# A gated state-space and expert layer on one core: adapter products on 128 rows, with mixed adapter values in unused rows of the down input

## What is computed

```
def _fused_linear(x, W, qa, qb, scale, w):
    out = x @ W.T
    a = jnp.einsum('th,krh->tkr', x, qa)
    b = jnp.einsum('tkr,khr->tkh', a, qb)
    mix = jnp.einsum('tkh,tk->th', b, w)
    return out + scale[None, :] * mix

def expert(muW, gW, gqa, gqb, gs, uW, uqa, uqb, us, dW, dqa, dqb, ds, w):
    xe = x + w @ muW.T
    gate = jax.nn.silu(_fused_linear(xe, gW, gqa, gqb, gs, w))
    up = _fused_linear(xe, uW, uqa, uqb, us, w)
    return _fused_linear(gate * up, dW, dqa, dqb, ds, w)
```

## Time and profile before

| | us |
|---|---|
| median of three runs | 1694.26 |
| lowest and highest run | 1688.27, 1695.64 |
| span of the profiled execution | 1685.8 |
| PE busy in it | 1568.4 |
| DVE busy | 1155.5 |
| POOL busy | 737.8 |
| ACT busy | 617.2 |

### The profile page before, as it was taken

How to read it: one execution, slowest core, us unless ns; L and a number is a source line. 1 busy time by engine, 2 the same in 40 slices (tenths; PEclk the granted TensorE clock), 3 DMA queues, 4 the chain that set the end, 5 groups by cost and what they waited for, 6 DMA issues and landing times.

```text
span 1685.8 us, 19547 instructions
## 1 busy us (share of the span) xinstructions
PE 1568.4 (93%) x6856; PEld 1155.1 (69%) x6856; DVE 1155.5 (69%) x1634; ACT 617.2 (37%) x971; POOL 737.8 (44%) x537
## 2 busy tenths in 40 slices
PE   3787799798888999999999999999999999999999
PEld 2343377566666677777777777777777777777776
DVE  5798964788999867487888755778888553333333
ACT  5545443444454434443343244333433321111111
POOL 4488510489898801077777301376786000000000
PEclk8799999899999999999999999999999999999999
DMA  7688627688787664765667445587665456566552
GB/s 251 215 285 315 254 80 253 201 290 297 270 289 286 253 255 172 248 228 205 232 238 258 152 161 196 202 275 257 238 208 180 175 200 210 184 222 222 195 181 85
DMA packets 111473, 375.87 MB, mean 223 GB/s; under 512 B 20176, under 2 KB 45776, under 8 KB 94864
## 3 DMA queue, kind: packets, MB, share of 16 engines
q1 hardware_dynamic: 101904, 340.81, 57.8%
q10 hardware_dynamic: 9472, 33.82, 5.8%
HBM read 304.33 MB, written 70.25 MB: 222 GB/s over the span
## 4 chain that ended last, share of the span: by engine, by line
PE 63%; DVE 18%; issue 5%; ACT 5%; POOL 4%; DMA 3%; SPq 0%; ACTq 0%; DVEq 0%; POOLq 0%
PE b_g L735 14%; PE b_u L735 14%; PE b_u L826 7%; DVE ring L1493 4%; PE b_g L826 3%; PE b_q L781 3%; PE b_q L826 3%; PE b_g L799 2%; DVE ring L1499 2%; PE b_g L766 2%; DVE tt L1467 2%; POOL ring L1392 2%; PE b_g L759 1%; POOL yx L1401 1%; DVE z L1467 1%
## 5 line engine op out<-in xcount | busy, mean ns | idle before, releaser
L1392 POOL TENSOR_TENSOR ring<-du,rep 128x512 f32<-128x512 f32 x256 | 344.5, 1349 | 151.4 <-DVE du L1571 91.9
L735 PE MATMUL b_g<-xnb,gm 128*128 128x512 f32 (+1 forms) x1440 | 356.2, 396 | 0.9 <-DVE xnb L1470 0.9
L735 PE MATMUL b_u<-xnb,gm 128*128 128x512 f32 (+1 forms) x1440 | 349.1, 391 | 0.0
L1493 DVE TENSOR_TENSOR_SCAN ring<-b_a,ring 128x512 f32<-128x512 f32 x256 | 310.8, 1214 | 15.7 <-ACT b_a L964 8.4
L1401 POOL TENSOR_TENSOR yx<-yx,ring 128x512 f32<-128x512 f32 x192 | 261.8, 1364 | 130.4 <-DVE ring L1499 129.9
L735 PEld LDWEIGHTS b_g<-xnb,gm 128*128 128x128 f32 (+1 forms) x1440 | 252.1, 179 | 89.1 <-issue 24.6
L735 PEld LDWEIGHTS b_u<-xnb,gm 128*128 128x128 f32 (+1 forms) x1440 | 257.1, 179 | 71.1
L1467 DVE SCALAR_TENSOR_TENSOR tt<-tt,b_g 128x512 f32<-128x512 f32 (+1 forms) x120 | 82.1, 684 | 222.7 <-ACT tt L964 222.5
L964 ACT ACTIVATE b_a<-delta,a_neg 128x512 f32<-128x512 f32 x256 | 173.6, 681 | 113.9 <-DVE ring L1493 113.9
L964 ACT ACTIVATE tt<-b_g 128x512 f32<-128x512 f32 (+1 forms) x120 | 71.1, 593 | 316.7 <-PE b_u L766 286.3
L826 PE MATMUL b_u<-dwt,hhl 128*128 128x512 f32 (+1 forms) x720 | 185.4, 394 | 0.0
(11 more groups left out here) (254 smaller groups left out, 2120.2 us busy)
## 6 DMA issues: line engine op xcount, KB each, us to landing
gm<-scr_gm SPq DMA_DIRECT2D x64, 1024.0 KB, 6.8
dwt<-scr_dw SPq DMA_DIRECT2D x32, 1536.0 KB, 6.8
rep<-bc_d ACTq DMA_DIRECT2D x64, 512.0 KB, 5.8
gm<-scr_gm SPq DMA_DIRECT2D x32, 768.0 KB, 4.4
dqt<-scr_dq SPq DMA_DIRECT2D x25, 896.0 KB, 9.1
scr_gm<-gm SPq DMA_DIRECT2D x20, 1024.0 KB, 7.5
scr_dw<-dwt SPq DMA_DIRECT2D x10, 1536.0 KB, 6.2
qat<-scr_qa SPq DMA_DIRECT2D x25, 512.0 KB, 10.2
```

The lines of the kernel that those rows point to most:

```text
L735: i = mm(out_b[0:IW[m], :], w, v, start=(n == 0), stop=(n == 11 and not is_routed(s)))
L1392: v.tensor_tensor(ring[:, T % NRING], du[:, T % 4, :], rep[:, N % NREP, 0], ALU.mult).then_inc(pool_dbu, 1)
L1493: v.tensor_tensor_scan(w, ba[T % 2][:], w, 0.0, ALU.mult, ALU.add).then_inc(dve_scan, 1)
```

## The change

The change touches four things.

- The adapter products take 128 rows. A new tile `awt` holds six operands: `a_g` and `a_u` with the high part of the adapter values in one half of the rows and the low part in the other, and (for two bodies in turn) `aw_g` and `aw_u` with the high part in one half and the routing weights `ws` in the other. `qbx` holds the matching weights: high parts in both halves, and low parts in one half with the mask's part in the other. Each tile m then has four products in place of four pairs. ACT rounds into two places at a time, in two operations; DVE takes the low part in two operations, into the other half of the rows.
- Of the 64 mixed values of the down adapter, the high and low parts of the second 32 go into rows 96 to 127 of `hh` and `hl`'s third tile, with the weights in the same rows of `dwt`, so that `down`'s third tile, on 128 rows in routed bodies, multiplies them too. The first 32 stay in `daw_s` on 96 rows, and `adapter_b` has one product for each bank.
- As `down`'s third tile now needs the mixed values, it moves behind the other tiles of all four banks. The next body's first `up` product moves ahead of it.
- Weights, stores and loads are cut to the new places; the mask's part is loaded into `qbx` (one buffer) and `gqa`; several small tiles are put into others to make room.

The diff, cut:

```diff
+        C0, C0B, C0C, C1 = (slice(k * 32, (k + 1) * 32) for k in range(4))
+        HID = slice(0, IW[2])
-        dwt, dqt = sb("dwt", [P, 2, RAW], F32R), sb("dqt", [P, 2, Q_D], F32R)
-        qat, qbt = sb("qat", [P, 2, HC * P], F32R), sb("qbt", [P, 2, I], F32R)
-        gqt = [sb("gqt%d" % k, [P, GQ], F32R) for k in range(2)]
+        dwt, dqt = sb("dwt", [P, 2, RAW], F32R), sb("dqt", [P, Q_ALL], F32R)
+        qat = sb("qat", [P, 2, HC * P], F32R)
+        qbx, gqa = sb("qbx", [P, 4, I], F32R), sb("gqa", [P, P], F32R)
...
+        awt = sb("awt", [P, 6, L], F32R)
+        a_g, a_u = awt[:, 0], awt[:, 1]
+        aw_g, aw_u = [awt[:, 2], awt[:, 4]], [awt[:, 3], awt[:, 5]]
...
             def gq_load(s):
                 r = rho(s)
-                if r >= 2:
-                    sp.wait_ge(pe_gu, IC * (body_of(r - 2) + 1))
-                sp.wait_ge(dma_gqs, 16 * NF)
-                sp.dma_start(gqt[r % 2][:].bitcast(F32), scr_gq[r % NF]).then_inc(dma_gq[r % 2], 16)
+                if r >= 1:
+                    sp.wait_ge(pe_gu, IC * (body_of(r - 1) + 1))
+                sp.dma_start(qbx[HALF:P, 2].bitcast(F32), scr_gq[r % NF][HALF:P, 0:I]).then_inc(dma_gq, 16)
+                sp.dma_start(qbx[0:HALF, 3].bitcast(F32), scr_gq[r % NF][0:HALF, 0:I]).then_inc(dma_gq, 16)
...
-            sp.dma_start(cs[:], cst).then_inc(dma_cst, 16)
-            sp.dma_start(inv_i[:], inv.partition_broadcast(NE)).then_inc(dma_cst, 16)
+            sp.dma_start(cs[:, 0:C_GW], cst[:, 0:C_GW]).then_inc(dma_cst, 16)
+            sp.dma_start(cs[:, C_GW:C_GW + 3], cst[:, C_GX:C_ALL]).then_inc(dma_cst, 16)
+            sp.dma_start(gw, cst[:, C_GW:C_GX].rearrange("p (c n) -> p c n", c=HC)).then_inc(dma_cst, 16)
+            sp.dma_start(inv_i, inv.partition_broadcast(NE)).then_inc(dma_cst, 16)
...
                     w_load(s + 1)
+                    gqa_load(s + 1)
+                    next_pieces(s + 1, ("qa", "gm0", "gm1", "gm2"))
                     gq_load(s + 1)
-                    next_pieces(s + 1, ("qa", "gm0", "gm1", "gm2", "qb"))
+                    next_pieces(s + 1, ("qb",))
...
-                g = gqt[r % 2]
-                for j, out_b in ((0, bg[m]), (1, bu[m])):
-                    rows = slice(j * HALF, (j + 1) * HALF)
-                    mm(out_b[0:IW[m], :], g[rows, cols], ws[rows, r % 2], start=False, stop=False)
-                if m == 0:
                     ready(pe, "qb", s)
                     pe.wait_ge(dve_awl, r + 1)
-                for k, (hl_, v) in enumerate(((0, aw_h), (0, aw_l), (1, aw_h))):
-                    for j, out_b in ((0, bg[m]), (1, bu[m])):
-                        rows = slice(j * HALF, (j + 1) * HALF)
-                        i = mm(out_b[0:IW[m], :], qbt[rows, hl_, cols], v[rows, :], start=False, stop=(k == 2))
+                for out_b, w, v in ((bg[m], 0, a_g), (bg[m], 2, aw_g[r % 2]), (bu[m], 1, a_u), (bu[m], 3, aw_u[r % 2])):
+                    i = mm(out_b[0:IW[m], :], qbx[:, w, cols], v, start=False, stop=(w >= 2))
                 return i
...
-                    k = slice(0, IW[m])
+                    k = slice(0, P if is_routed(s) else IW[m])
...
-                mm(down_bank(s, tc)[:], daw_s[:, t], dqt[:, 0, q], start=False, stop=False)
-                mm(down_bank(s, tc)[:], daw_s[:, t], dqt[:, 1, q], start=False, stop=True
-                   ).then_inc(pe_dn, 1)
+                mm(down_bank(s, tc)[:], daw_s[HID, t], dqt[HID, QA:Q_D], start=False, stop=True).then_inc(pe_dn, 1)
...
-                up_waits(s, 0)
-                up(s, 0, 0)
+                if e == 0:
+                    up_waits(s, 0)
+                    up(s, 0, 0)
...
-                down(s, 0, (2,))
-                down(s, 1, (2,))
-                down(s, 2)
+                down(s, 2, (0, 1))
+                down(s, 3, (0, 1))
                 if post:
                     xn_transposed(b + 1, (2, 3))
-                down(s, 3)
+                if e < NF - 1:
+                    up_waits(s + 1, 0)
+                    up(s + 1, 0, 0)
+                pe.wait_ge(dve_daw, rho(s) + 1)
+                pe.wait_ge(act_daw, 3 * (rho(s) + 1))
                 for tc in DONE:
+                    down(s, tc, (2,))
                     adapter_b(s, tc)
...
+                if kind == "qb":
+                    rounded(qbx[0:HALF, 0], src[0:HALF, 0:I])
+                    rounded(qbx[HALF:P, 1], src[HALF:P, 0:I])
+                    rounded(qbx[HALF:P, 0], src[0:HALF, 0:I])
+                    rounded(qbx[0:HALF, 1], src[HALF:P, 0:I]).then_inc(act_hi[slot_of[k]], 1)
+                    return
...
-                rounded(aw_h, aw[:]).then_inc(act_aw, 1)
+                k = r % 2
+                for rows, g_ in ((slice(0, HALF), 0), (slice(HALF, P), 1)):
+                    rounded(awt[rows, g_:g_ + 3 + 2 * k:2 + 2 * k],
+                            aw[rows].unsqueeze(1).broadcast_to([HALF, 2, L])).then_inc(act_aw, 1)
 
             def daw_round(s):
                 act.wait_ge(dve_dawf, rho(s) + 1)
-                rounded(rnd[:], dawf[:]).then_inc(act_daw, 1)
+                rounded(daw_s[:], dawf[:]).then_inc(act_daw, 1)
+                rounded(hh[C1, 2], dawf[C1]).then_inc(act_daw, 1)
+                act.wait_ge(act_daw, 3 * rho(s) + 1)
+                rounded(daw_s[C0B], dawf[C0]).then_inc(act_daw, 1)
...
+                if kind == "dw":
+                    lo(dwt[:, 1, 0:2 * H], src[:, 0:2 * H], dwt[:, 0, 0:2 * H])
+                    lo(dwt[HID, 1, W2], src[HID, W2], dwt[HID, 0, W2]).then_inc(done, 1)
+                    return
+                if kind == "dq":
+                    lo(dqt[:, Q_D:Q_ALL], src[:, 0:QA], dqt[:, 0:QA])
+                    lo(dqt[C0B, QA:Q_D], src[C0, QA:Q_D], dqt[C0, QA:Q_D])
+                    lo(dwt[C1, 1, W2], src[C1, QA:Q_D], dqt[C1, QA:Q_D]).then_inc(done, 1)
+                    return
+                if kind == "qb":
+                    src = raw[slot_of[k]]
+                    lo(qbx[0:HALF, 2], src[0:HALF, 0:I], qbx[0:HALF, 0])
+                    lo(qbx[HALF:P, 3], src[HALF:P, 0:I], qbx[HALF:P, 1]).then_inc(lo_done[slot_of[k]], 1)
+                    return
...
-                dve.wait_ge(act_aw, rho(s) + 1)
-                lo(aw_l, aw[:], aw_h).then_inc(dve_awl, 1)
+                dve.wait_ge(act_aw, 2 * (rho(s) + 1))
+                lo(awt[HALF:P, 0], aw[0:HALF], awt[0:HALF, 0])
+                lo(awt[0:HALF, 1], aw[HALF:P], awt[HALF:P, 1]).then_inc(dve_awl, 1)
...
-                stt(daw_s[:], rnd[:].bitcast(F32), mlo[:], dawf[:], ALU.mult, ALU.add).then_inc(dve_daw, 1)
+                r = rho(s)
+                dve.wait_ge(act_daw, 3 * r + 1)
+                lo(daw_s[C0C], dawf[C0C], daw_s[C0C])
+                dve.wait_ge(act_daw, 3 * r + 2)
+                lo(hl[C1, 2], dawf[C1], hh[C1, 2]).then_inc(dve_daw, 1)
```

More of the change, by code:

```diff
@@ L87, in gated_ssm_moe @@
         sb("pr_rest", [P, 2 * PRE_ALL - 2 * RAW])
-        scr = {k: dram("scr_" + k, [NX if k[0] == "g" or k == "dw" else NF, P, 2 * width[k]]) for k in tile_of}
+        scr = {k: dram("scr_" + k, [NX if k[0] == "g" or k == "dw" else NF, P, Q_ALL if k == "dq" else 2 * width[k]])
+               for k in tile_of}
         scr_pr = dram("scr_pr", [P, 2 * PRE_ALL])
@@ L300, in scaled, with stored, loaded @@
             return 2 * (s - 3) + (1 if kind == "qb" else 2)
+        def stored(kind):
+            return 32 if kind in ("qb", "dw", "dq") else 16
+        def loaded(kind):
+            return 64 if kind == "qb" else 16
         def stored_before(kind, s):
@@ L320, in ready @@
             if from_scratch(s):
-                eng.wait_ge(dma_t[kind], 16 * loads(kind, s))
+                eng.wait_ge(dma_t[kind], loaded(kind) * loads(kind, s))
             elif s == 0:
@@ L408, in load @@
                 free(sp, kind, s)
-                sp.wait_ge(dma_st[kind], 16 * stored_before(kind, s))
+                sp.wait_ge(dma_st[kind], stored(kind) * stored_before(kind, s))
+                if kind == "dw" and s >= NX:
+                    sp.wait_ge(dma_st["dq"], stored("dq") * NF)
+                if kind == "dq":
+                    sp.dma_start(dqt[:].bitcast(F32), scr[kind][w_index(s)]).then_inc(dma_t[kind], 16)
+                    return
+                if kind == "qb":
+                    at = scr[kind][w_index(s)]
+                    both = at[:, 0:I].rearrange("(j p) i -> p j i", j=2)
+                    for rows in (slice(0, HALF), slice(HALF, P)):
+                        sp.dma_start(qbx[rows, 0:2].bitcast(F32), both).then_inc(dma_t[kind], 16)
+                    sp.dma_start(qbx[0:HALF, 2].bitcast(F32), at[0:HALF, I:2 * I]).then_inc(dma_t[kind], 16)
+                    sp.dma_start(qbx[HALF:P, 3].bitcast(F32), at[HALF:P, I:2 * I]).then_inc(dma_t[kind], 16)
+                    return
                 sp.dma_start(tile_of[kind][:].bitcast(F32).rearrange("p a n -> p (a n)"), scr[kind][w_index(s)]
@@ L797, in adapter_a @@
                 n = 3 * m
```

(21 more changed lines are left out.)

151 lines of the change are left out of this document (101 added, 50 removed).

## The result

The changed kernel takes 1752.13 us (median of 4 runs, 1751.73 to 1756.65); the kernel before, on the same chip, 1693.73 (1688.27 to 1695.64). The ratio is 1.0363, 95% interval 1.0339 to 1.0387: slower by 58 us, where 18 were forecast and the range ended at 1736.

A forecast was written before the change was run, and what follows sets the result against it. PE was taken to bound item 3 and ordinary bodies of items 1 and 2, DVE item 0. Terms -17.4 (item 3), -5 (items 1 and 2), +39 (item 0), +1.5 (start) gave +18: median 1712 us, range 1672 to 1736.

The forecast's parts named there:

- PE's gain in item 3: Last batch item, no scan running: PE saves 1.26 us of seams and 0.91 of mixed-value products per body; -17.4 over eight.
- the fourth rival: Products on 96 rows beside products on 128 bring their own seam, so the 1.26 us is not gained: 1730, chance 0.05.
- Items 1 and 2: Batch items with the next item's scan woven in: -2.5 us per item, -5 for two.
- The walk by sections: DVE's loop through an ordinary body of items 1 and 2, summed by sections to 32.2 us before added operations.
- the price of the added operations: Two added DVE operations per body in items 1 and 2: 1.14 plus 0.6 x 2.2, with ACT's 0.3, 2.75 us.
- the bare price: Added DVE operations without meeting POOL: 1.14 us per body in items 1 and 2, 2.3 in item 0.
- "all blocked": Every added DVE operation meets POOL and pays 1.1 us more: +7 for items 1 and 2 together, +58 for item 0.
- the bare sum: Items 1 and 2 if added operations cost only their own length: -24 us for both, ordinary body 33.6.
- Item 0: First batch item, weights also split, DVE the bound: six more DVE operations in each of six bodies, 6.3 us each; +39.
- the cover of ACT's roundings: Item 0: rounding of the adapter's second matrix ends about when DVE asks; up to 0.6 us per body, upper end only.
- The start: Two more issues ahead of the first item's rows, +1, and first-scan DVE operations, +0.5: +1.5 us (0 to 3).
- The third: Rival: POOL meets all added operations and ACT's rounding comes late as well: +51 us, 1745, chance 0.08.

The follow-up runs named there:

- with POOL cut: Both kernels with POOL's two scan operations of the second to fourth batch item cut from 512 to 32 columns: before 1674.00 us, changed 1685.08 us.
- The single-operation run: Changed kernel with the mixed values' low part made by one DVE operation on rows 64 to 127 instead of two on 32 rows each: 1746.34 us.
- its swap on ACT: The 1746.34 us kernel with ACT's four roundings of the next body's second adapter matrix ahead of its three of the mixed values: 1732.71 us.
- the run of the mixed values alone: Mixed values' part and new PE order only, adapter products as in the kernel before (pairs on 64 rows): 1709.18 us, ratio 1.0099.
- With the old order on PE: Changed kernel with the next body's first up product put back to the start of its own body: 1827.94 us, ratio 1.0814.

## Why the prediction was wrong

- **The direction was right, and PE's gain in item 3** (2.0 us per body, 2.2 put). A body of item 3 was to take 33.3 us and takes 33.49. PE waits neither for the mixed values nor for the adapter's matrix, so the order holds and the cover of its load was rightly put at nothing. From the chain through that body, answering:

```profile
1585.66 0.68 PE b_u L886 x3
1586.34 0.23 PE b_u L893
...
1592.12 0.46 PE b_g L826 x2
```

Products on 128 rows take their 0.23 each, and one on 96 rows between them has no seam, so the fourth rival falls.

- **Items 1 and 2 had the wrong sign** (-5 for both, measured +20). The walk by sections can be checked against the body shown above. First to second gating operation: 6.79 put, 6.76 measured. Second to third: 6.41 put, 6.14. Third to the multiplication: 7.92 and the pair's 1.56 (0.60, six tenths of 1.1, 0.3 of ACT), 9.5 put, 10.83 measured. Multiplication to the end of the mixed values' low part: 4.25 put, 4.81 measured in this body (its own second piece took 1.68). From there to the next gating operation: 8.0 put, 8.4. The order was read rightly; the step that failed is **the price of the added operations**. Six tenths of 2.2 us were put per body for meeting POOL; POOL took 2.3, so every body paid in full. The sentence that POOL "runs dry behind several such operations" was the wrong one here: POOL has two operations ready at the pair and one at the mixed pieces, and no more are needed. The first of the pair pays as well, which in the earlier trace rows it did not: DVE now waits 0.50 us for ACT ahead of it, and POOL's operation (859.38) has begun before DVE's (859.80). In all, DVE's work in item 1 rose from 203.24 to 229.28 us, 3.7 per body, where 1.14 (the bare price) and 1.32 (POOL) were put; with POOL cut it rose by 1.6. Counted one for one over seven bodies, this makes some 9 of the 12.5 us by which item 1 was missed.

  Even the "all blocked" sum, +7 for both items, is 13 short. The runs with POOL cut show a second step that failed, **the overlap with PE**: there the change gave 4 us per item, not the 12 of the bare sum (10, if ACT's 0.3 per body, which the -24 leaves out, is counted). In the kernel before DVE still waited 19 us for ACT's tanh in item 1, in the changed one 3.4: the operations and their round trips to ACT used up that time, and PE then waited for DVE. What the walk left out are the waits of PE that come with the new order, 11.6 us in item 1 for the multiplication and 5.7 for the mixed values; with POOL cut 4.8 us of the former remain. Over item 1 PE's busy time fell by 9.2 us (246.61 to 237.38), where seven times 2.2 make 15.4, and its idle time rose by 19.3 (1.6 to 20.9). Behind a wait PE is slow as well: the twelve products of 863.57 take 4.58 us, at a granted clock of 0.63. What this adds to the time was not separated.

- **Item 0** (+39 put, +55 measured). Six bodies were to take 6.3 us more each and take 8.5, 50.3 on average where 48 to 50 were named. The whole six, first before, then after:

```profile
327.41:578.59 251.18, 223.57 (x974) 163.91 (x973) 230.05 (x269) 117.55 (x179) 220.17 (x150) 0.98 0.82 288
```

```profile
336.31:638.40 302.09, 228.77 (x876) 171.45 (x876) 273.45 (x304) 149.19 (x226) 224.35 (x151) 0.91 0.69 232
```

DVE's work rose by 43.4 us, 7.2 per body, and its idle time by 1.3. With POOL cut its work rises by 3.1 per body, so contention adds 4.2: **six in ten of 6.6, 4.0, was right here.** What was short are the bare price, 2.3 put for 3.1, and **the cover of ACT's roundings**, taken at nothing with "up to 0.6" at the upper end: DVE waits 5.2 us for the second adapter matrix and 3.0 for the adapter values in these six bodies (1.4 for the former matrix before), 1.1 per body. The single-operation run and its swap on ACT show that wait and its price. The rest was put at +1.3 (the first expert's 3.5 less PE's 2.2 in the last); the last of the seven stretches alone cost 4.0, and the last expert's weights are split in it too. The first expert's work ahead of its multiplication lies in the stretch of the start, so these two rows of the table do not match the forecast's terms exactly.

- **The start** (+1.5 put, +8.9 in the profiles). In the first scan the two pieces of the small down matrix and the operation behind them meet POOL:

```profile
116.80 1.31 DVE L1566 TENSOR_TENSOR dqt<-xx,dqt 32x512 fp32r<-32x512 f32 x1 [0.90 <-ACT dwt L1024]
118.12 1.40 DVE L1566 TENSOR_TENSOR dwt<-xx,dqt 32x512 fp32r<-32x512 f32 x1
119.55 1.64 DVE L1563 SCALAR_TENSOR_TENSOR z<-dawf,z 128x512 f32<-128x512 f32 x1
```

With the wait 5.3 us, where the kernel before has the last of the three alone, at 0.69. That looks like an accident of timing: in the run of the mixed values alone the two pieces take 0.68 and 0.69. Across the seven profiles with the changed kernel's start, the first multiplication comes at 329.4 to 337.0 us, with the start of before at 327.4 and 330.1. What moved the other microseconds was not separated.

- **The rivals.** The third (all met, and ACT late, 1745) came nearest, and its two conditions are what the runs show in items 1 and 2 (every added operation but the first mixed piece is met, and DVE waits 0.50 us for ACT, 0.3 put); in item 0 not all is met. That its sum came so near is in part luck: it gave items 1 and 2 +7, where +20 came, and item 0 +58, where +55 came. It was given 8 in 100, because the rate of meeting was thought of as one number for the whole kernel.

## What to carry to other kernels

Before work is moved from the engine that is the bound to one at 70 to 80%, count its operations, not their length, and ask of each one where its inputs lie: here one input in PSUM for SBUF, with a swap on PE, was worth 23 us. An operation that is added beside a loaded neighbour pays wherever that neighbour has something ready, and one that is removed can hand part of its price to others, as the small down matrices did here (2.8 us of 3.8 came back). An operation that is cut into pieces for a layout also brings a round trip to the engine that prepares each piece; the half of this change that could be had without more operations was the half that paid.

## What had not been expected of the hardware

A DVE operation on 32 rows took as long as one on 128 (0.68 us), and the time around it was longer. In item 1 of the changed kernel with POOL cut:

```profile
754.43 0.68 DVE L1567 TENSOR_TENSOR daw_s<-dawf,daw_s 32x512 fp32r<-32x512 f32 x1
755.13 0.69 DVE L1567 TENSOR_TENSOR hhl<-dawf,hhl 32x512 fp32r<-32x512 f32 x1
755.85 1.22 DVE L1605 TENSOR_TENSOR_SCAN ring<-b_a,du 128x512 f32<-128x512 f32 x1
```

They start 0.70 and 0.72 us apart, behind each other's ends, where operations on all rows start 0.60 apart with the same length (794.61 and 795.21). By the Trainium skill ("VectorE: DVE Perf Modes", Two Vector instructions with no wait between them) an instruction whose operands begin in another group of 32 partitions than the last one's starts only when all earlier ones have finished. The trace agrees, and puts it at 0.10 us. A wait between the two operations is not the reason: the adapter pair has none and takes 1.39 us for two of 0.69 in item 3 (1578.79), and the two of the earlier trace rows have one between them. The 0.10 may be part of the 0.8 us by which item 0's bare price was short.

In item 0 the granted clock fell from 0.98 to 0.91 over the six bodies, and PE's busy time rose, 223.57 to 228.77, with a tenth fewer products. The twelve that follow PE's wait of 4.92 us take 5.23 us, at a granted clock of 0.54, so for the most part at the lower of the two levels (1.2 GHz); twelve of the same line without a wait ahead take 2.91 at 1.00, the upper one (2.4 GHz; 851.08 in item 1). With the old order on PE, and more waits, it was 0.88 over these six bodies.
